# Lane numbers of the destination masks read from a PSUM bank in a graph network on one core

## The reference

```python
# layer 0: sum of the neighbours' normalised rows
neigh = jax.ops.segment_sum(node_feats[src], dst, num_segments=n)
h = (1.0 + eps) * node_feats + neigh
...
# layer 2: messages of 8 blocks of 64, summed by destination
xg0, xg1 = y0[edge_src], y1[edge_src]
mid0 = w_a * xg0 * ea0
mid1 = w_b * jnp.einsum('euc,ec->eu', xg1, ea1) * INV_SQRT3
mid2 = (w_c * xg0)[:, :, None] * ea1[:, None, :]
mid3 = (w_d * ea0)[:, :, None] * xg1
mids = jnp.concatenate([mid0, mid1, mid2.reshape(-1, 3 * MUL), mid3.reshape(-1, 3 * MUL)], axis=1)
agg = jax.ops.segment_sum(mids, edge_dst, num_segments=n)
```

## Time and profile before

| | us |
|---|---|
| median of 3 runs (2610.39 to 2612.98) | 2612.69 |
| the profiled execution | 2612.01 |
| its span | 2610.3 |
| POOL busy in the span | 1181.3 (45%) |
| DVE busy | 1134.2 (43%) |
| TensorE busy | 1971.4 (76%) |
| neighbour sum: first to last gather issued | 184.2 to 776.1 |
| message stage: first to last gather issued | 1440.5 to 2111.0 |

### The profile page before, as it was taken

The page is one execution under the profiler, slowest core; times in us unless marked ns, Lnnn a source line. Parts: engine busy times, 40 slices in busy tenths (PEclk is TensorE's granted clock), DMA queues, the critical chain, the costliest instruction groups (busy, mean ns, idle before and its releaser), DMA issues. The chain is left out here.

```text
span 2610.3 us, 37725 instructions
## 1 busy us (share of the span) xinstructions
PE 1971.4 (76%) x10704; PEld 1611.1 (62%) x10704; DVE 1134.2 (43%) x2352; ACT 1016.5 (39%) x3203; POOL 1181.3 (45%) x1138
## 2 busy tenths in 40 slices
PE   0018888888868875999505588888888888978998
PEld 0015555555535655999405478777778775547997
DVE  3523333333331256222274677777777753121111
ACT  0004444444403520332224466666666634522332
POOL 0017777777760001555200777777777720002222
PEclk9958999999968855999757799999999999988999
DMA  2236767676630022999511566666666612016563
GB/s 75 77 120 191 227 208 226 208 225 210 213 119 17 0 82 88 348 350 351 191 59 43 159 188 190 185 187 189 187 187 188 187 53 86 20 26 205 196 199 110
DMA packets 268851, 415.76 MB, mean 159 GB/s; under 512 B 63063, under 2 KB 158026, under 8 KB 268246
## 3 DMA queue, kind: packets, MB, share of 16 engines
q1 hardware_dynamic: 213530, 261.19, 31.3%
q0 software_dynamic: 54784, 150.09, 19.1%
q10 hardware_dynamic: 390, 2.76, 0.3%
HBM read 327.54 MB, written 87.39 MB: 159 GB/s over the span
## 5 line engine op out<-in xcount | busy, mean ns | idle before, releaser
L1798 POOL DMA_INDIRECT msg_got<-y_dram,pair_src x464 | 529.5, 1141 | 227.3 <-issue 135.0
L694 POOL DMA_INDIRECT sum_got<-xn_dram,pair_src x464 | 450.9, 972 | 192.7 <-issue 136.8
L1811 ACT ACTIVATE msg_scaled<-msg_plain,msg_w 128x125 f32<-128x125 f32 x1392 | 416.0, 386 | 261.1 <-DVE msg_plain L1846 247.4
L734 PE MATMUL sum_ps_sum<-sum_got,sum_onehot 128*125 128x256 f32 x928 | 267.3, 415 | 100.1 <-DMA sum_got<-xn_dram,pair_src 99.7
L734 PEld LDWEIGHTS sum_ps_sum<-sum_got,sum_onehot 128*125 128x125 f32 x928 | 181.3, 203 | 249.6 <-issue 204.9
L1828 PE MATMUL msg_ps_z<-msg_prod,msg_plain 128*125 128x256 f32 x928 | 246.4, 388 | 110.6 <-ACT msg_scaled L1811 59.2
L1837 PEld LDWEIGHTS msg_ps_z<-msg_prod,msg_scaled 128*125 128x125 f32 x2320 | 290.8, 188 | 13.2
L1298 ACT ACTIVATE ffn_run_hid<-ffn_run_ps_h,cols 128x128 f32<-128x128 f32 x512 | 145.8, 368 | 390.2 <-PE ffn_run_ps_h L1247 390.2
L1837 PE MATMUL msg_ps_z<-msg_prod,msg_scaled 128*125 128x128 f32 x2320 | 292.3, 273 | 0.0
L793 DVE TENSOR_TENSOR agg<-sum_ps_sum,agg 125x256 f32 x232 | 98.6, 425 | 385.7 <-PE sum_ps_sum L734 385.7
L1247 PEld LDWEIGHTS ffn_run_ps_h<-ffn_run_rows_t,ffn_run_w 128*128 128x128 f32 x2048 | 246.6, 194 | 8.7 <-DVE ffn_run_rows_t L1332 3.5
(11 more groups left out here) (291 smaller groups left out, 2477.2 us busy)
## 6 DMA issues: line engine op xcount, KB each, us to landing
ffn_run_w<-in_L_ffn_w SPq DMA_DIRECT2D x128, 512.0 KB, 6.3
msg_w<-edge_w SPq DMA_DIRECT2D x232, 260.0 KB, 3.7
edge_w<-sum_wide SPq DMA_DIRECT2D x52, 1040.0 KB
ffn_run_w<-in_L_ffn_Wd SPq DMA_DIRECT2D x32, 1024.0 KB, 5.6
sum_got<-xn_dram,pair_src POOLq DMA_INDIRECT x464, 3.3
msg_got<-y_dram,pair_src POOLq DMA_INDIRECT x464, 3.7
xn_dram<-xn SPq DMA_DIRECT2D x10, 625.0 KB
ffn_combine_got<-ffn_results SPq DMA_DIRECT2D x10, 625.0 KB
```

The costliest lines, as they stand in the source:

```text
L694: pool.indirect_dma_start(got[:, n % RING, u, :], None, k.xn_dram, bass.IndirectOffsetOnAxis(ap=k.pair_src[:, n, u:u + 1].bitcast(U32), ax ...
L734: last = pe.matmul(ps_sum[n % ZB][0:P, :], onehot[n % OB][:, u, :], got[:, n % RING, u, :], start=(u == 0), stop=(u == KC - 1))
L1798: pool.indirect_dma_start(got[:, s % RS, c, :, :].rearrange("p k v -> p (k v)"), None, k.y_dram, bass.IndirectOffsetOnAxis(ap=k.pair_src[: ...
L1811: last = act.activation(scaled[s % MB][:, x, c, :], plain[s % MB][:, c, :], ACT.Copy, scale=w[:, s % RS, c, D + x:D + x + 1])
```

## The change

In both stages a bank of PSUM, `ps_lanes`, is filled once, by a matmul of a row of ones (one partition of `onesf`) with the row of lane numbers (one partition of `iota`), so that each of its 128 partitions holds 0 to 124. DVE waits for it once, and all masks read the lane numbers from there instead of from SBUF. `pair_dst` is still read from SBUF. For the bank, the neighbour sum has 3 sum buffers instead of 4, and the message stage 6 instead of 8.

```diff
@@ def sum_neighbours(nc, k):
-    RING, OB, ZB, WB, RB = 12, 4, 4, 2, 6
+    RING, OB, ZB, WB, RB = 12, 4, 3, 2, 6
...
+        ps_lanes = ph.ps("lanes", [128, P])
+        lanes_made = ph.sem("lanes_made")
...
+            pe.matmul(ps_lanes[:, :], k.onesf[0:1, :], k.iota[0:1, 0:P], start=True, stop=True).then_inc(lanes_made, 1)
             pe.wait_ge(fc_in, 16 * 10)
...
+            dve.wait_ge(lanes_made, 1)
             for n in range(NPAIR):
 
                 if n >= 1:
                     dve.wait_ge(added, n)
-                dve.tensor_tensor(onehot[n % OB][:, :, :], k.iota[:, 0:P].unsqueeze(1).to_broadcast([128, KC, P]),
+                dve.tensor_tensor(onehot[n % OB][:, :, :], ps_lanes[:, :].unsqueeze(1).to_broadcast([128, KC, P]),
                                   k.pair_dst[:, n, :].unsqueeze(2).to_broadcast([128, KC, P]), ALU.is_equal).then_inc(masked, 1)
@@ def sum_messages(nc, k):
-    RS, MB, ZB = 4, 3, 8
+    RS, MB, ZB = 4, 3, 6
...
+        ps_lanes, lanes_made = ph.ps("lanes", [128, P]), ph.sem("lanes_made")
...
         def _(pe):
+            pe.matmul(ps_lanes[:, :], k.onesf[0:1, :], k.iota[0:1, 0:P], start=True, stop=True).then_inc(lanes_made, 1)
             pe.wait_ge(zeroed, 2)
...
-                dve.tensor_tensor(plain[s % MB][:, :, :], k.iota[:, 0:P].unsqueeze(1).to_broadcast([128, CH, P]),
+                dve.tensor_tensor(plain[s % MB][:, :, :], ps_lanes[:, :].unsqueeze(1).to_broadcast([128, CH, P]),
...
+            dve.wait_ge(lanes_made, 1)
             mask(0)
```

## The result

| | before | changed |
|---|---|---|
| median of 4 runs, us | 2611.54 (2609.40 to 2612.98) | 2576.05 (2572.11 to 2581.44) |
| ratio, 95% interval | | 0.9865 (0.9847 to 0.9883) |
| profiled execution, us | 2612.01 | 2574.42 |
| its span, us | 2610.3 | 2572.7 |
| neighbour sum, first to last gather started | 591.0 | 579.1 |

The change makes the kernel 35.5 us faster. I had forecast 21.4 us less, 2591.3, and the range ended at 2577: the direction was right, the measured time lies 15 us under the forecast and 1 us under the range.

A forecast was written before the change was run, and what follows sets the result against it. POOL's gathers were taken to bound both stages. The terms -6.4 - 13.9 - 0.8 - 0.3 = -21.4 us took the profiled 2612.0 to 2590.6, and the median, 0.7 above, to 2591.3 us; range 2577 to 2606.

The forecast's parts named there:

- What bounds the stages: Both stages: POOL's gathers set the pace, with a floor of 1.245 us per gather.
- What lengthens a gather: Both stages: a gather reading under a DVE instruction with two SBUF inputs is held to its end; masks hold 6.4, 19.2 us.
- rival D: Both stages: holds have another cause that only coincides with DVE's instructions (the DMA queue); 2612.7 us, chance 0.04.
- Neighbour sum, -6.4: Neighbour sum: all holds are by masks, so all 6.4 us go and every gather takes the floor.
- Message stage, -13.9 between 8.7 and 19.2: Message stage: 116 steps become like those without a mask's hold, -13.9 us; 8.7 from ten such in a row, 19.2 subtracting holds.
- the 64 steps without a mask's hold: Message stage: of 111 four-gather steps before the change, 64 had no mask's hold and lasted 5.549 us on average.
- Rival C: Message stage: all 19.2 us go over to the products, only the sum and heads gain 7.5; 2605 us, chance 0.13.
- Masks' length, buffers: Both stages: masks reading PSUM keep their length, and fewer sum buffers add no wait; zero each.
- The heads, -0.8 and -0.3: Stage starts: message stage -0.8 us, as DVE starts later and the fourth gather is held, not the third; neighbour sum -0.3.
- B: Message stage: the rhythm gets shorter still, to 5.44 us a step, 26.6 us there; 2578.6 us, chance 0.15.
- F: Message stage: gathers fall into a rhythm where two products each hold one, costing 24.5 us; 2629.7 us, chance 0.04.
- E: Both stages: an instruction with a PSUM and an SBUF input still keeps POOL out in this form; 2612.7 us, chance 0.04.

The follow-up runs named there:

- e10: Changed kernel with the two products of 768 elements in halves, faster conditions: 2548.9 us against 2614.5 for the kernel before, 0.9749.
- e11: Changed kernel with all products cut to 256 elements, eight instructions instead of three: 2531.4 us against 2614.8 for the kernel before, 0.9682.
- e8: Changed kernel with the two products of 768 elements in halves, slower conditions: 2758.9 us against 2838.4 for the kernel before, 0.9727.
- e9: Changed kernel, only the mask behind each memset of agg reading iota in SBUF, faster conditions: 2597.1 us against 2614.5 for the kernel before, 0.9936.
- e3: Kernel before with only the sum buffers cut, 4 to 3 and 8 to 6: 2838.0 us against 2840.8, 0.9989.
- e1: Kernel before plus DVE's wait for its memset of agg in both stages: 2822.5 us against 2840.8, 0.9933.
- e4: Kernel before plus a one-column copy behind each memset of agg, no wait: 2820.1 us against 2840.8, 0.9923.
- e2: Changed kernel, only the mask behind each memset of agg reading iota in SBUF, slower conditions: 0.9989 of the kernel before.
- e7: Changed kernel, only the mask behind each memset of agg reading iota in SBUF, slower conditions, repeated: 0.9986 of the kernel before.
- e6: Repeat of the kernel before plus DVE's wait for its memset of agg in both stages: 2823.1 us against 2838.4, 0.9947.

## Why the prediction was wrong in size

- *What bounds the stages:* right. POOL never stops in either, and the span fell by what the gathers gave up.
- *What lengthens a gather:* right for the steady part. Of 50 gathers that read under a mask of the message stage after the change, from the 17th on, none was held. e10 and e11 show the same rule from the other side: the shorter the instruction with two SBUF inputs, the shorter the hold, but for the 17th gather of e8 and e10. The Trainium skill's SBUF — State Buffer, section Who interferes with whom, has both rules that I weighed. The one on two SBUF inputs agrees with these traces (48 holds by masks with two such inputs, none with one). Its inference that `tensor_tensor` leaves descriptor generation alone does not hold for these gathers (rival D): products alone still hold them for 62.9 us.
- *Neighbour sum, -6.4:* measured -5.9.
- *Message stage, -13.9 between 8.7 and 19.2:* measured -12.2, and -8.2 in e9, just short of the lower bound. The step that I took from the 64 steps without a mask's hold, 5.549 us, came out as 4 x 621.5 / 447 = 5.56, so the step was right. Rival C had a share: 6 of the 18.7 us went to the products.
- *Masks' length, buffers:* zero and zero, right as far as seen (418 and 670 ns; no wait of TensorE for an addition, and e3).
- *The heads, -0.8 and -0.3:* this is the step that failed. "it is held by the memset of `agg` ... and then by mask(1)": I put a hold of 12.8 us (5.5 in the neighbour sum) down to the memset, which the change does not touch, and only its last 0.3 to 0.5 us to the mask. But the whole hold hangs on the mask: a memset of the same length holds nothing once the mask behind it has an input in PSUM, or a wait or a one-column copy stands between (e1, e4), and the hold is back with that one mask's SBUF inputs (e9). The heads gave 5.8 + 14.7 = 20.5 us instead of 1.1, and that is more than the miss. The rows had a hint: I had seen that the memset has no SBUF input, which the rule for holds asks for, and still named it as the holder. That the third gather read at 1443.17, and the memset is recorded from 1445.25 only, proves less than it seems: gap and record together are 6.67 us for 6400 elements and 13.34 for 12800, the same for each element, so the gap may be the memset's own.
- *The sum:* the steady terms were 20.3 us and came to 18.1; without the heads the forecast would have been 2 us off. I had costed the heads as a shift of the same hold from one gather to the next, never as its end.
- *Rivals:* B's number, 2578.6, came near, which is luck: the reason isn't B's, as the rhythm did not get shorter than 5.55. F, D and E did not occur.

## What to carry to other kernels

Where POOL's gathers set the pace, look at each DVE instruction with two SBUF inputs beside them: put one input in PSUM, or cut it into pieces, as far as DVE's idle time pays for them; here halves of the long products alone gave 32 us, and pieces of 256 together with the change 83. Put no such instruction right behind a long memset: a wait for the memset, or one small instruction between, frees every gather under it. And name the holder of a long wait by the rule that was found for the short ones.

## What the runs showed of the hardware that was not expected

A DVE instruction with two SBUF inputs right behind a long memset keeps a gather out from before the memset's record begins to its own end: 5.8 and 13.3 us. With a wait (e1), a one-column copy between (e4), or one input in PSUM (the changed kernel), nothing is held. That the instruction reads ahead is my reading of it; the traces show only when the gathers stand.

A hold ends with the DVE instruction under way, also where the next one has two SBUF inputs (156 of 157 in e10). The exception, 1.81 us through four instructions at the 17th gather of e8 and e10, is not explained.

The same kernel ran 8.6 to 8.8% slower under conditions that the record doesn't name (2838 to 2841 us against 2611.5 to 2614.8). Its gathers' packets ended as soon after their start as at the faster ones; TensorE's steps in the message stage were longer (6.18 us against 4.99, at a granted clock of 0.92 against 1.00 in the steady part), and POOL waited for its ring. What makes the steps longer was not found, nor why halved products shorten them. There the steady part of this change can't be told from nothing (e2, e7), and the heads are worth 15 to 21 us (e1, e4, e6), about as under the faster conditions.
